# Last attention of a four-layer kernel: one early query part moved behind the stage's barrier, and the first loads cut in two waves

## The reference

```
def _L3_xattn_ref(query, key, value, mask, Wq, bq, Wk, bk, Wv, bv, Wo, bo):
    B, S, D, H = (2, 512, 256, 16)
    DK = D // H
    Q = query @ Wq.T + bq
    K = key @ Wk.T + bk
    V = value @ Wv.T + bv
    ...                                   # split into 16 heads of 16
    scores = jnp.einsum('bhqd,bhkd->bhqk', Q, K) / jnp.sqrt(jnp.float32(DK))
    scores = jnp.where(mask == 0, -jnp.inf, scores)
    weights = jax.nn.softmax(scores, axis=-1)
    attn = jnp.einsum('bhqk,bhkd->bhqd', weights, V)
    return attn.transpose(0, 2, 1, 3).reshape(b, -1, D) @ Wo.T + bo
x = x + _L3_xattn_ref(_layernorm(x), ctx_1024, ctx_1024, mask_1x1xSxS2_ik0, ...)
x = x + _L3_ffn_ref(_layernorm(x), ...)
```

## Time and profile before

| | us |
|---|---|
| median of 3 runs (2519.26 to 2524.21) | 2519.31 |
| the profiled execution | 2509.91 |
| its span, first to last instruction | 2507.6 |
| PE busy in the span | 2266.9 (90%) |
| DVE busy | 1701.8 (68%) |
| ACT busy | 1286.0 (51%) |

### The profile page before, as it was taken

One profiled execution on the slowest core, in us unless ns is written; L12 is line 12 of the kernel. 1 busy time (PEld: TensorE's weight loads), 2 busy tenths in 40 slices (PEclk: granted clock), 3 DMA queues, 4 the chain that ended last, 5 costly groups with the idle time before them and its releaser, 6 DMA issues.

```text
span 2507.6 us, 35628 instructions
## 1 busy us (share of the span) xinstructions
PE 2266.9 (90%) x13660; PEld 1200.6 (48%) x13660; DVE 1701.8 (68%) x3546; ACT 1286.0 (51%) x1732; POOL 157.3 (6%) x198
## 2 busy tenths in 40 slices
PE   8999999999567769999989999776999999999888
PEld 3333333333312356777656777563444444443387
DVE  4778877886589744351752443766799999997385
ACT  3555555565178621223632223630687777877753
POOL 1000000000045520000000000001000000000011
PEclk9999999999678779999989999895899999998898
DMA  4000000000131152200011111003210111010232
GB/s 133 5 6 9 10 10 5 10 10 10 48 138 66 54 180 77 86 6 11 3 47 40 58 61 46 1 27 87 56 25 12 36 18 30 2 35 2 75 126 70
DMA packets 63218, 108.46 MB, mean 43 GB/s; under 512 B 13210, under 2 KB 44839, under 8 KB 62023
## 3 DMA queue, kind: packets, MB, share of 16 engines
q1 hardware_dynamic: 61190, 101.48, 13.1%
q0 software_dynamic: 1536, 4.20, 0.5%
q10 hardware_dynamic: 322, 0.50, 0.1%
HBM read 87.88 MB, written 17.73 MB: 42 GB/s over the span
## 4 chain that ended last, share of the span: by engine, by line
PE 77%; DVE 12%; ACT 5%; issue 3%; DMA 3%; POOL 0%; ACTq 0%; SPq 0%; DVEq 0%; POOLq 0%
PE PS L2655 9%; PE PS L2635 8%; PE PS L1498 7%; PE PS L638 7%; PE PS L2597 4%; PE PS L618 2%; PE PS L1454 2%; PE PS L571 2%; PE PS L1477 2%; PE PS L1479 2%; PE PS L1478 2%; PE PS L586 2%; PE PS L622 2%; PE PS L376 2%; PE PS L625 2%
## 5 line engine op out<-in xcount | busy, mean ns | idle before, releaser
L2758 DVE TENSOR_REDUCE pm<-PS 128x1 f32<-128x512 f32 x768 | 473.1, 682 | 51.4 <-PE PS L2597 50.4
L2719 ACT ACTIVATE P<-PS 128x1024 f32<-128x1024 f32 (+1 forms) x416 | 422.0, 1023 | 119.9 <-PE PS L2635 117.3
L2597 PE MATMUL PS<-Ks,Qs 49*128 49x512 f32 x768 | 302.6, 481 | 31.7 <-DMA Qs<-q_parts 25.2
L2635 PE MATMUL PS<-Qs,Ks 51*128 51x512 f32 (+1 forms) x832 | 309.4, 459 | 0.4 <-ACT P L2719 0.4
L714 ACT ACTIVATE P<-PS 128x1024 f32<-128x1024 f32 (+1 forms) x208 | 213.3, 1026 | 168.6 <-PE PS L625 168.6
L2655 PE MATMUL PS<-P,V 128*17 128x256 f32 (+2 forms) x3072 | 261.5, 413 | 8.2 <-ACT P L2719 7.3
L638 PE MATMUL PS<-P,V 128*64 128x512 f32 (+1 forms) x832 | 225.1, 619 | 2.2 <-ACT P L714 2.2
L798 DVE TENSOR_TENSOR acc<-acc,P 128x1024 f32<-128x1024 f32 (+1 forms) x176 | 214.2, 1217 | 2.4 <-ACT P L714 0.2
L2635 PEld LDWEIGHTS PS<-Qs,Ks 51*128 51x128 f32 (+1 forms) x832 | 127.1, 185 | 171.4 <-issue 139.2
L2597 PEld LDWEIGHTS PS<-Ks,Qs 49*128 49x128 f32 x768 | 127.3, 194 | 66.1 <-DVE pm L2758 31.9
L1038 PE MATMUL PS<-ind,sel 128*8 128x512 bf16 (+3 forms) x288 | 82.5, 403 | 47.4 <-DVE ind L1147 23.4
(11 more groups left out here) (363 smaller groups left out, 4563.3 us busy)
## 6 DMA issues: line engine op xcount, KB each, us to landing
mi<-in_mask SPq DMA_DIRECT2D x32, 800.5 KB, 4.4
We<-in_L_ffn_w SPq DMA_DIRECT2D x16, 1024.0 KB, 7.2
Wg<-gate_rows SPq DMA_DIRECT2D x8, 1024.0 KB, 13.0
Qs<-q_parts SPq DMA_DIRECT2D x90, 64.0 KB, 3.5
Ks<-k_parts SPq DMA_DIRECT2D x24, 200.1 KB, 6.0
R<-denominators SPq DMA_DIRECT2D x30, 128.0 KB, 2.8
q_parts<-T SPq DMA_DIRECT2D x5, 512.0 KB, 2.8
k_parts<-Tk SPq DMA_DIRECT2D x6, 400.0 KB, 2.7
```

Of the source, the lines that this page charges most:

```text
L2597: m = e.matmul(PS[:, b, :], self.Qs[rows, s, pr, q0:q0 + 128], self.Ks[rows, s, pr, cs], start=True, stop=not masked)
L2635: m = e.matmul(ps, self.Ks[rows, s, pr, ks], self.Qs[rows, s, pr, q], start=True, stop=not masked)
L2719: e.activation(self.P[0:r, n % 4, :, :], PS[0:r, b:b + 2, :], ACT.Exp, scale=0.25).then_inc(*k.ac_exp.up((3, n)))
L2758: e.tensor_reduce(self.pm[:, u % 2, i, c:c + 1], PS[:, ring.of(("max", key)), :], AX.X, ALU.max).then_inc(*k.dv_max.up((3, *key)))
```

## The change

Three things, all at the seam of F2 and A3. First, part (0,2) leaves F2 and becomes a step inside A3, after the loads; it now uses tile `T` and the three banks of A3, and the query loads of chunk 2 follow it. Second, "key stack" and "query stack" take a range of pairs: group 0 is loaded in a first wave (pair 0) and a second (pair 1), each of six key DMAs of 16 x 1601 on SP and six query DMAs of 16 x 512 on ACT. Third, the rows load is split: one mask row and one row of ones for slot 0, pair 0 (1 x 1601 each) go first on each queue, and the rest goes behind the second wave. The very first maxima (u = 0, pair 0) wait for the first wave alone, on semaphores of its own; all others wait for everything, as before.

```
-        self.early, self.ring2 = [(0, 0), (0, 1), (0, 2)], ring2
+        self.early, self.ring2 = [(0, 0), (0, 1)], ring2
...
-        out = [(self, "begin", ()), (self, "rows load", ())] + self.key_loads(0)
-        out += self.query_loads(0, 0) + [(self, "value load", ()), (self, "load", ())]
-        rest = self.norms.steps(6, 3) + self.query_loads(0, 1) + self.query_loads(0, 2)
-        rest += [(self, "part", (0, 3))] + self.query_loads(0, 3)
+        first, second = slice(0, 1), slice(1, 2)
+        out = [(self, "begin", ()), (self, "first rows load", ())] + self.key_loads(0, first) + self.query_loads(0, 0, first)
+        out += self.key_loads(0, second) + self.query_loads(0, 0, second) + [(self, "rows load", ())]
+        out += [(self, "value load", ()), (self, "load", ())]
+        rest = self.norms.steps(6, 3) + self.query_loads(0, 1)
+        for c in range(2, 4):
+            rest += [(self, "part", (0, c))] + self.query_loads(0, c)
...
+        if first:
+            ld = self.ld_row_first[o]
+            e.dma_start(Ks[o:o + 1, 0, :], row).then_inc(*ld.up("mask", 16))
+            e.dma_start(Qs[o:o + 1, 0, 0:M], ones[0:1, :]).then_inc(*ld.up("all", 16))
+            return
         ld = self.ld_row[o]
-        e.dma_start(Ks[o:o + 1, :, :], wide(row, M)).then_inc(*ld.up("mask", 16))
-        e.dma_start(Ks[o + 1:o + 3, :, :], wide(ones, M)).then_inc(*ld.up("ones", 16))
-        e.dma_start(Qs[o:o + 1, :, 0:M], wide(ones[0:1, :], M)).then_inc(*ld.up("q", 16))
-        e.dma_start(Qs[o:o + 1, :, M:N], wide(ones[0:1, :], N - M)).then_inc(*ld.up("all", 16))
+        e.dma_start(Ks[o:o + 1, 1:4, :], wide(row, M, 3)).then_inc(*ld.up("mask", 16))
+        e.dma_start(Ks[o + 1:o + 3, :, :], wide(ones, M, 4)).then_inc(*ld.up("ones", 16))
+        e.dma_start(Qs[o:o + 1, 1:4, 0:M], wide(ones[0:1, :], M, 3)).then_inc(*ld.up("q", 16))
+        e.dma_start(Qs[o:o + 1, :, M:N], wide(ones[0:1, :], N - M, 4)).then_inc(*ld.up("all", 16))
...
+            if (u, pr) == (0, 0):
+                for o in (48, 112):
+                    at.wait_ge(self.ld_row_first[o], "all")
+                at.wait_ge(self.ld_k_first, (0, 1, 2))
+                at.wait_ge(self.ld_q_first, (0, 1, 2))
...
-            elif n > 4:
+            elif n > 3:
                 at.wait_ge(*self.stored(self.parts[n - 2]))
...
-    out.append(("F2", row3.load_steps() + ffn2.order() + [(att3, "part", (0, 2))]))
+    out.append(("F2", row3.load_steps() + ffn2.order()))
```

More of the change, by code:

```diff
@@ L2387, in __init__ @@
         self.ld_row = {o: k.new(f"ld_row3_{o}") for o in (48, 112)}
+        self.ld_row_first = {o: k.new(f"ld_row3_first{o}") for o in (48, 112)}
+        self.ld_k_first, self.ld_q_first = k.new("ld_ks_first"), k.new("ld_qs_first0")
         self.ld_nm = [k.new(f"ld_nm3{i}") for i in range(2)]
@@ L2405, in rows_steps, with key_loads, query_loads @@
         return [(self, "rows", (u,)), None, None, (self, "turn", (u,))]
[L2407 to L2411, removed]
+    def key_loads(self, g, pairs=slice(0, 2)):
+        return [(self, "key stack", (g, hh, blk, pairs)) for hh in range(2) for blk in range(3)]
+    def query_loads(self, g, c, pairs=slice(0, 2)):
+        return [(self, "query stack", (g, c, hh, blk, pairs)) for hh in range(2) for blk in range(3)]
     def divide_steps(self, u):
@@ L2490, in tile, with rows_load @@
         return self.T_early[:, :, :] if key in self.early else self.T[:, self.parts.index(key) % 2, :, :]
-    def rows_load(self, e, at, o):
+    def rows_load(self, e, at, o, first):
         k = self.k
@@ L2495, in rows_load @@
         row, ones = self.row.row[0:1, :].bitcast(F32), self.row.row[32:34, :].bitcast(F32)
[L2496 removed]
+        wide = lambda x, n, times: x[:, 0:n].unsqueeze(1).to_broadcast([x.shape[0], times, n])
         Ks, Qs = (x[:].bitcast(F32).rearrange("p s r n -> p (s r) n") for x in (self.Ks, self.Qs))
+        if first:
[3 more added lines that the diff above has]
+            return
         ld = self.ld_row[o]
[L2499 to L2502 removed]
+        e.dma_start(Ks[o:o + 1, 1:4, :], wide(row, M, 3)).then_inc(*ld.up("mask", 16))
+        e.dma_start(Ks[o + 1:o + 3, :, :], wide(ones, M, 4)).then_inc(*ld.up("ones", 16))
+        e.dma_start(Qs[o:o + 1, 1:4, 0:M], wide(ones[0:1, :], M, 3)).then_inc(*ld.up("q", 16))
+        e.dma_start(Qs[o:o + 1, :, M:N], wide(ones[0:1, :], N - M, 4)).then_inc(*ld.up("all", 16))
     def query_stack(self, e, at, key):
         k = self.k
[L2506 removed]
+        g, c, hh, blk, pr = key
         s, cs = g % 2, slice(512 * c, 512 * c + 512)
+        ld = self.ld_q_first if (g, c, pr) == (0, 0, slice(0, 1)) else self.query_loaded(g, c)[0]
         at.wait_ge(*self.stored((g // 2, c)))
@@ L2529, in sync @@
             e.dma_start(self.V[0:65, 12, :], self.keys.vd[1536:M, :]).then_inc(*self.ld_v.up("all", 16))
-        elif step == "rows load":
-            self.rows_load(e, at, 112)
+        elif step in ("first rows load", "rows load"):
+            self.rows_load(e, at, 112, step == "first rows load")
         elif step == "part":
@@ L2534, in sync @@
         elif step == "key stack":
-            g, hh, blk = key
+            g, hh, blk, pr = key
             s = g % 2
+            ld = self.ld_k_first if (g, pr) == (0, slice(0, 1)) else self.ld_k[s]
             for p in self.keys.parts:
@@ L2592, in tensor @@
             b = ring.take(at, ("max", key))
[L2593 to L2596, removed]
+            if (u, pr) == (0, 0):
[3 more added lines that the diff above has]
+                at.wait_ge(self.ld_q_first, (0, 1, 2))
+            else:
+                for o in (48, 112):
+                    at.wait_ge(self.ld_row[o], "all")
+                at.wait_ge(self.ld_k[s], (g, 1, 2))
+                at.wait_ge(*self.query_loaded(g, u % 4))
             m = e.matmul(PS[:, b, :], self.Qs[rows, s, pr, q0:q0 + 128], self.Ks[rows, s, pr, cs], start=True,
@@ L2698, in scalar @@
                          bias=self.row.bq[:, half:half + 1]).then_inc(*k.ac_proj.up((3, "q", *key)))
-        elif step == "rows load":
-            self.rows_load(e, at, 48)
+        elif step in ("first rows load", "rows load"):
+            self.rows_load(e, at, 48, step == "first rows load")
         elif step == "query stack" and key[:2] == (0, 0):
```

8 lines of the change are left out of this document (4 added, 4 removed).

## The result

| | before | after |
|---|---|---|
| median, first timing | 2520.88 (6 runs) | 2507.51 (6 runs), ratio 0.9946, interval 0.9928 to 0.9963 |
| median, second timing | 2517.78 (23 runs) | 2505.19 (12 runs), ratio 0.9959, interval 0.9934 to 0.9984 |
| profiled execution, its span | 2509.91, 2507.6 | 2501.06, 2499.2 |

The change makes the kernel faster: by 13.4 us in the first timing; in the second by 10.3 (0.0041 of 2517.8, interval 4 to 17 us), or 12.6 between the medians. I had forecast 5.5. 2507.51 is also just inside the lower end of my range, where rival A lay (2509.4).

What follows compares the result with a forecast made beforehand. The prediction took A3's opening chain, behind a 25.2 us wait for first loads, as the bound. Terms -9.8 (first matmul -14.7, 4.9 lost to ACT) and +4.3 summed to -5.5 us: median 2519.3 to 2513.8, range 2507.5 to 2518.5.

Steps and rivals of the forecast that it cites:

- rival A: At the seam, ACT's row issues are not held longer than before; -9.9 us, median 2509.4; chance 0.27.
- part (0,2) out of F2, at the barrier: At the barrier ending F2, A3's first issue starts at about 1684.3 instead of 1688.66: -4.4 us.
- first matmul, all together: At A3's start, earlier barrier, fewer first rows and halved loads bring the first matmul from 1709.5 to 1694.8: -14.7 us.
- ACT late at the reciprocal: Before the fourth reduction, DVE's reciprocal waits for ACT's square root; 4.9 of the 14.7 us are lost.
- part (0,2) inside A3: Among A3's maxima, the part costs 3.52 us of DVE idling plus 0.75 of DVE work: +4.3 us, nothing hiding it.
- What is late next: ACT: On ACT's queue, held row issues free ACT at 1703.9 (bounds 1699.5 and 1705.7), reciprocal at 1704.1: -9.8 us.
- First wave: Half of group 0's keys and queries, 792 KB, land 8.1 us after 1686.3; 1694.8 taken, against 13.1 us before.
- Rival B: In A3's first loads, the first wave is no shorter, first matmul at 1699.4; -4 to -6 us, median about 2514.6; chance 0.12.
- a single row on a single DMA engine: For A3's first rows, four single rows share one DMA engine, making the first matmul 0.8 us later.
- At nothing: In A3, later value load, later query loads and remaining rows cost nothing, new semaphores under 0.3 us; no clock gain.
- Rival C: On ACT, row issues are held longer, value load possibly between, reciprocal 1710.2; +0.6 us, median 2519.9; chance 0.07.
- rival D: At the barrier, something other than the store decides, first issue stays at 1688.7; -1.1 us, median 2518.2; chance 0.06.

Runs made afterwards that it cites:

- e3: Changed kernel with group 0's keys and queries loaded in one wave, rows still split; first matmul 16.94 us after DVE's last write of X, first score 70.11.
- e6: Changed kernel with ACT also issuing SP's four remaining row DMAs; ACT free 1.94 us later than in the changed kernel, first score 1.71 us later.
- e1: Kernel before the change with only part (0,2) moved behind the barrier, loads as before; ratio 0.9994 to the kernel before (2515.93 against 2517.78 us).
- e7: Changed kernel with part (0,2) and the last normalization before the first maxima, second-wave queries issued by SP; first score 56.82 us after DVE's last write of X.
- e8: As e7, with part (0,3) also put before the first maxima; 2498.55 us, ratio 0.9922 to the kernel before the change.
- e9: Changed kernel with the DMA writing ones into two rows of Ks issued as two one-row DMAs; ACT free 14.37 us after DVE's last write of X.
- e5: Changed kernel with the two-row ones DMA last of each queue's four remaining row DMAs; ACT free 3.3 us earlier, reciprocal only 0.19 us earlier.

## Why the prediction was wrong

The direction, the place and most steps were right; one term was mis-sized, and it decided the number. Step by step, from DVE's last write of X:

| step | forecast | measured |
|---|---|---|
| part (0,2) out of F2, at the barrier | -4.4 | -4.05 |
| first matmul, all together | -14.7 | -15.06 (second profile -14.38) |
| ACT late at the reciprocal | +4.9 | +0.23 (second profile +0.33) |
| part (0,2) inside A3 | +4.3 | +4.28 |
| sum at the first score | -5.5 | -10.56 (second profile -9.77) |

The first row is contained in the second; the sum is of the last three.

"ACT late" is how much farther the reciprocal lies behind the first matmul than before: 4.62 less 4.39 in the first profile, 4.72 less 4.39 in the second.

**The failed step** is "What is late next: ACT", its choice of "ACT free at 1703.9", taken near an upper bound of 1705.7. Counted from X that is +19.7; measured were +14.58 and +15.36. The lower bound, 1699.5 or +15.3, was the right one. I had read the 2.8 us issues as waiting for row data that moves slowly, and reasoned that behind a second wave of keys it would move later still and hold the issues longer. The first half was not contradicted by the earlier trace rows (a share of 0.17 and 26 GB/s are also what row data moving slowly would give); the second half rested on no row, since none showed a row issue behind a backlog. The runs show that the hold does not grow with the backlog: in after the third and fourth issue were held 2.35 and 2.44 us behind both waves, where it had been 2.79 and 2.74 with no load in front, and in e3 no issue was held with the engines full. ACT's four remaining row issues took 6.4 us in all (1694.59 to 1700.95), not 12. e6 shows that the chain does follow ACT one for one once ACT is late. So rival A is what happened, at -10.6 where I had -9.9, although by the letter of its sign (`rstd` within a us of its input) it just missed: the input lay 1.10 us before `rstd`, 1.19 in the second profile.

**Barrier and part.** Right in both terms within 0.4 us, and their sum is close to nothing, as said: 0.9994 when timed alone. That e1's loads take 1.2 to 1.9 us longer was not foreseen.

**First wave.** First query issue to first matmul 7.66 us (8.1 worked out, 8.5 taken), from 13.3. Rival B, that a halved wave lands no sooner, is out. The rule of the Trainium skill that spoke for it ("DMA: Bandwidth & Descriptors", "Rules for kernel authors"), that small transfers should be merged, did not decide here: with twelve loads of 32 KB and twelve of 100 KB the DMA engines moved 182 GB/s over 1690 to 1694, against 129 in e3's stretch of the merged loads, and the merged form had its first matmul 6.7 us later. The rule counts bytes per transfer; here the chain waited for the first half of them. The other rule of the Trainium skill in the prediction, a single row on a single DMA engine, was not tested by any run.

**At nothing.** Right. The 25th maximum waited for DVE and not for rows or keys; the value load was issued at 1700.92 and its first use is at 1755.1. PE's granted clock was 0.50 over 1697 to 1719 and 0.58 over 1719 to 1741, and each part took its 3.78 us again. Rival C needed a reciprocal later than 1709.6, and rival D a first issue at 1688.7 or +4.4; neither came.

**What the forecast left aside:** 12 us of idle PE. I had priced part (0,2) in two places, in F2 and among the maxima, and both cost about 4 us. In the third place, between barrier and first data, its matmuls delay nothing, as e7's and e8's traces show; its piece on DVE delays the normalization there, and still the first score of e7 is 7.0 us earlier than after's, part and normalization together.

**Open.** What holds the row issues. It is not the DMA engines' load (e3), not the two-row form (e9), and not the number of row DMAs on the queue alone (e6: eight issues on ACT with two held, before: four with two held). In e5 it was mostly gone when the two-row DMA went last (0.95 us for ACT's last issue, 1.44 for SP's). Whether a row DMA in front must be moving its data for the hold, no run separates. Also open is where the 2.8 us are by which the first timing exceeds the trace; its interval reaches from 9 to 18 us, and the ratio of the second timing does not repeat them.

## What to carry to other kernels

Where a stage opens with a barrier and a wait for loads, cut the first load to what the first instructions read, with semaphores of its own, and send the rest behind it; then look for work whose inputs are there at the barrier and put it in front of the wait. Moving the same work from one side of a barrier to the other gains nothing when the chain continues on both. And when an issue is held for microseconds and the cause is not known, carry the hold over as it is: here it stayed near 2.4 us behind a second wave, and the forecast failed by letting it grow with a backlog that no row had shown to matter.

## What the runs showed of the hardware

- An issue of a row DMA takes 0.6 to 0.8 us or is held for 0.9 to 2.9, with no relation to the DMA engines' share that these runs show: 2.79 us at a share of about 0.2 (before), 2.35 at 1.05 (after), 0.71 at 1.01 (e3).
- The first row issue on ACT after the barrier takes longer than SP's: 1.52 against 0.70 us in after, 1.20 against 0.73 in before.
- The same 327 matmuls took 37.2 us at a granted clock of 0.95 and 40.2 at 0.87, in two executions of one kernel. Read from one profile each, such a difference would be put down to an edit.
